# A fused transformer block on one core: two operand stacks filled by halves, feed-forward buffers of their own, distances over 120 quarters

## The reference, cut to what matters

```python
x = x + attn_a(layernorm(x))   # att1: 3 coordinates per token, scores = -distance/4, causal softmax over keys, @ V
x = x + ffn(layernorm(x))      # ffn2: sigmoid(xr Wr) * (relu(xk Wk)^2 Wv), xr and xk mix a token with the one before
x = x + attn_b(layernorm(x))   # proj3 + attention: 16 heads of 16, causal softmax(q k / 4) v
x = x + ffn(layernorm(x))      # ffn4: the same weights as ffn2
```

## Time and profile before

| | us |
|---|---|
| three runs | 2085.45, 2093.70, 2105.44 |
| median | 2093.70 |
| profiled execution, its own time | 2109.85 |
| its span, first to last instruction | 2108.1 |
| PE, DVE, ACT, POOL busy | 1849.2, 1467.0, 1323.7, 728.2 |
| granted clock of TensorE, mean | 0.943 of full speed |

### The profile page before, as it was taken

The page is one execution under the profiler, slowest core; times in us unless marked ns, Lnnn a source line. Parts: engine busy times, 40 slices in busy tenths (PEclk is TensorE's granted clock), DMA queues, the critical chain, the costliest instruction groups (busy, mean ns, idle before and its releaser), DMA issues. The chain is left out here.

```text
span 2108.1 us, 32379 instructions
## 1 busy us (share of the span) xinstructions
PE 1849.2 (88%) x9842; PEld 922.5 (44%) x9842; DVE 1467.0 (70%) x4288; ACT 1323.7 (63%) x2585; POOL 728.2 (35%) x879
## 2 busy tenths in 40 slices
PE   5677898889997999889998899979998899988986
PEld 4453443335543455434543355434544345322423
DVE  5576778767676677667786667766776677768642
ACT  3564355876569565776758665695657766455664
POOL 1342332234333253333443243333532334312313
PEclk8797899999998999999999899989999999989998
DMA  3006113111131112410132111311124101322000
GB/s 85 1 23 123 26 56 67 31 31 32 55 76 31 31 31 82 80 21 12 41 110 42 31 31 56 76 31 31 34 83 76 22 11 41 99 33 50 13 21 20
DMA packets 64346, 97.26 MB, mean 46 GB/s; under 512 B 15655, under 2 KB 58029, under 8 KB 58030
## 3 DMA queue, kind: packets, MB, share of 16 engines
q1 hardware_dynamic: 64174, 95.20, 20.2%
HBM read 61.09 MB, written 33.55 MB: 45 GB/s over the span
## 5 line engine op out<-in xcount | busy, mean ns | idle before, releaser
L973 ACT ACTIVATE pt<-exp_bank 128x512 f32<-128x512 f32 (+1 forms) x1216 | 698.9, 582 | 526.6 <-PE exp_bank L935 521.0
L989 DVE CUSTOM_DVE_ANT_0 max_bank<-max_bank,mask 128x128 f32<-128x128 f32 (+3 forms) x1024 | 501.8, 500 | 400.9 <-PE max_bank L922 386.4
L922 PE MATMUL max_bank<-ks,qs 96*128 96x512 bf16 (+3 forms) x1536 | 523.5, 346 | 85.9 <-DVE piece_max L992 44.9
L935 PE MATMUL exp_bank<-qs,ks 98*128 98x512 bf16 (+3 forms) x1536 | 515.4, 342 | 40.0 <-ACT pt L973 37.0
L992 DVE TENSOR_REDUCE piece_max<-max_bank 128x1 f32<-128x512 f32 x512 | 344.1, 686 | 94.4 <-PE max_bank L922 90.2
L954 PE MATMUL o_bank<-pt,v 128*17 128x512 f32 (+3 forms) x3072 | 334.1, 508 | 13.7 <-POOL pt L1011 11.0
L922 PEld LDWEIGHTS max_bank<-ks,qs 96*128 96x128 bf16 x1536 | 150.9, 99 | 399.5 <-DVE piece_max L989 140.9
L1011 POOL TENSOR_SCALAR_AFFINE_SELECT pt<-pt 128x512 f32<-128x512 f32 x256 | 171.5, 670 | 412.6 <-ACT pt L973 411.8
L935 PEld LDWEIGHTS exp_bank<-qs,ks 98*128 98x128 bf16 x1536 | 152.4, 100 | 236.0 <-ACT pt L973 118.5
L633 PE MATMUL side<-vp,p 128*128 128x260 f32 x576 | 171.4, 423 | 28.7 <-ACT p L560 21.0
L412 ACT ACTIVATE xh<-xs,shift,rstd 128x256 f32<-128x256 f32 x256 | 149.7, 596 | 47.8 <-POOL shift L401 47.8
(11 more groups left out here) (119 smaller groups left out, 2348.4 us busy)
## 6 DMA issues: line engine op xcount, KB each, us to landing
parts_dram<-parts SPq DMA_DIRECT2D x64, 384.0 KB, 2.6
qs<-parts_dram SPq DMA_DIRECT2D x192, 128.0 KB, 7.2
ks<-parts_dram SPq DMA_DIRECT2D x32, 384.0 KB, 4.7
xs<-in_L_attn_a_x_dram SPq DMA_DIRECT2D x16, 512.0 KB, 4.2
ks<-parts_dram SPq DMA_DIRECT2D x32, 256.0 KB, 5.4
out_dram<-xs SPq DMA_DIRECT2D x16, 512.0 KB, 3.1
ks<-parts_dram SPq DMA_DIRECT2D x32, 128.0 KB, 5.8
qs<-neg_maxT SPq DMA_DIRECT2D x64, 8.0 KB, 1.9
```

Source lines behind the costliest of these rows:

```text
L922: pe.matmul(max_bank[u % MAX_BANKS][:, 0:k1 - k0], qs[r][0:KROWS, j, P * tile:P * (tile + 1)], ks[r][0:KROWS, j, k0:k1], start=True, stop= ...
L935: mm = pe.matmul(exp_bank[k % EXP_BANKS][:, (q1 - q0) * slot:(q1 - q0) * (slot + 1)], ks[r][:, j, P * kt:P * (kt + 1)], qs[r][:, j, q0:q1] ...
L973: act.activation(pt[:, e % 2, j + 1 - heads:j + 1, 0:w], exp_bank[k % EXP_BANKS][:, 0:heads * w].rearrange("p (j n) -> p j n", j=heads), A ...
L989: dve.tensor_tensor_reduce(scores, scores, mask[:, HALF - w:HALF], 1.0, LOWEST, ALU.add, ALU.max, piece_max[:, j, m:m + 1]).then_inc(max_f ...
```

## The change

It touches the table, the memory and the DMA queue at once.

- **Two stacks** in place of three. A stack's halves (tokens 0 to 511 and 512 to 1023) are loaded apart, by nine DMAs of half the size each, the first half 16 quarters ahead of the group, the second at its first quarter; PE waits for them at pieces 0 and 4. A run of contiguous bytes in DRAM falls from 8192 to 1024.
- **Maxima by halves**: PE's transposes, DVE's negation and copy and the DMAs come twice per group, after piece 3 and after piece 11, and each half takes eight DMAs in place of one pair for the whole (512 in place of 64). `LEAD` falls from 14 pieces to 12.
- **Feed-forward buffers**: `shifted` (three tensors), and `tm` also holds the gate. The waits between distances and feed-forward go; in their place the first Exp of the gate waits for `x_added`, Relu for the products of the half before.
- **A fourth x buffer**; x is stored and loaded at piece 13 of two turns later (before: 35 of one turn later).
- **The table**: att1 begins 66 quarters earlier, its distances take 120 quarters (`LONG`) from item 2 on; ffn4 begins at 168 in place of 82, but at 82 in the last turn. `XT_BEFORE` gives the wait for the transposed x in the new order. By `place()`, in the steady turn: ffn4 at quarters 4 to 34, ffn2 at 76 to 113, values and positions at 100 to 124, `project` at 139 to 167, distances and `attend` from 116 to 53 of the next turn.
- `p1` is shorter, with a wait before its front is used again. The rows of ones in the stacks are set by POOL instead of DVE. For item 1 the third square is ACT's instead of DVE's.

```diff
-STACKS = 3
+STACKS = 2
-LEAD = NP + 2
+LEAD = NP
-X_BUFFERS = 3
+X_BUFFERS = 4
-ATT1, FFN2, FFN4, PROJ3 = -44, 50, 82, 114
+ATT1, FFN2, FFN4, PROJ3 = -110, 52, 168, 110
+LAST_FFN4 = 82
...
+STACK_AT = [4 * (LEAD - 2 * NP + 2 * TPH), 4 * (LEAD - NP)]
...
-        STAGES += [(TURN * (n - 1) + FFN4, "ffn4", n - 2, 0)]
+        STAGES += [(TURN * (n - 1) + (FFN4 if n < B else LAST_FFN4), "ffn4", n - 2, 0)]
...
-PIECE_TIME = [2 + (q1 - q0) // P for _, q0, q1 in KEY_PIECES] + [5, 5, 5]
-PIECE_AT = [34 + sum(PIECE_TIME[:p]) for p in range(NP + 4)]
+SHORT = [2 + (q1 - q0) // P for _, q0, q1 in KEY_PIECES] + [5, 5, 5]
+LONG = [4 + 2 * (q1 - q0) // P for _, q0, q1 in KEY_PIECES] + [6, 6, 6]
+
+
+def piece_time(n, p):
+    return (SHORT if n < 2 else LONG)[p]
...
-    rows = [(4 * NP * (g + 1) + 1, ("maxima", g)) for g in range(GROUPS)]
+    rows = [(4 * (NP * g + (NP if h else TPH)) + 1, ("maxima", g, h)) for g in range(GROUPS) for h in range(2)]
...
+        shifted = [sb(f"shifted{k}", [P, NC, HALF]) for k in range(3)]
...
-                    if p == 0 and n > 1:
-                        act.wait_ge(tm_ready, 2 * halves_before("att1", n, 0))
...
-                    elif s == "ffn2":
-                        pool.wait_ge(p1_exp, NP * (n + 1))
...
                 if f > 0:
-                    act.wait_ge(ka_ready, 2 * f - 1 + j)
+                    act.wait_ge(v_full, 2 * f)
...
-                r = th[:, 2 * j:2 * j + 2, :]
+                r = tm[:, 2 * j:2 * j + 2, :]
                 if k == 0:
-                    if f > 0:
-                        act.wait_ge(tm_ready, 2 * f - 1 + j)
+                    if f == 0:
+                        act.wait_ge(setup_taken, 5)
+                    else:
+                        act.wait_ge(x_added, 2 * f - 1 + j)
...
             if n > 1:
-                sp_stack(NG * n)
+                for h in range(2):
+                    yield STACK_AT[h] + 4 * NP * NG * n
+                    sp_stack(NG * n, h)
...
-        def sp_stack(group):
+        def sp_stack(group, half):
...
+            lo, hi = HALF * half, HALF * (half + 1)
             if group >= STACKS:
-                nc.sync.wait_ge(s_full, EXP_PER_GROUP * (group - STACKS + 1))
+                nc.sync.wait_ge(s_full, exp_before(NP * (group - STACKS) + (2 * TPH if half == 0 else NP)))
...
-                    to[HD * slot:HD * (slot + count), :, :],
-                    src[kq, ht, part:part + count].rearrange("r d h n -> (r d) h n")[:, h0:h0 + GH, :]
-                ).then_inc(stack_ready[r], 16)
+                    to[HD * slot:HD * (slot + count), :, lo:hi],
+                    src[kq, ht, part:part + count].rearrange("r d h n -> (r d) h n")[:, h0:h0 + GH, lo:hi]
+                ).then_inc(stack_ready[r][half], 16)
...
-                    pe.wait_ge(crow_ready, 32 * (g + 1))
+                    pe.wait_ge(crow_ready, 256 * g + 128)
+                if m == TPH and j == 0:
+                    pe.wait_ge(crow_ready, 256 * g + 256)
...
-            if j == 0 and early == 0 and STACKS <= g < GROUPS and (g % NG or g == NG):
-                sp_stack(g)
+            for half in range(2):
+                g, early = divmod(u - STACK_AT[half], 4 * NP)
+                if early == 0 and STACKS <= g < GROUPS and (g % NG or g == NG):
+                    sp_stack(g, half)
...
             for c in range(2):
-                nc.sync.dma_start(qs[r][KROWS + c:KROWS + c + 1, :, :], neg_maxT[:, c, :]
-                                  ).then_inc(crow_ready, 16)
+                for j in range(GH):
+                    nc.sync.dma_start(qs[r][KROWS + c:KROWS + c + 1, j, HALF * h:HALF * (h + 1)],
+                                      neg_maxT[TPH * j:TPH * (j + 1), c, :]).then_inc(crow_ready, 16)
...
-            for r in range(STACKS):
-                yield SETUP_AT[7] + 12 + 8 * r
-                dve.memset(ks[r][KROWS:SROWS, :, :], 1.0).then_inc(rows_of_ones, 1)
...
+            pool.wait_ge(shift_ready, 2)
+            for r in range(STACKS):
+                pool.memset(ks[r][KROWS:SROWS, :, :], 1.0).then_inc(rows_of_ones, 1)
...
-                body = {"att1": [dve_att1(at, n)] + ([dve_squares(at, n)] if n < 2 else []), "proj3": [dve_proj3(at, n), dve_values3(at, n)]}.get(s, []) if h == 0 else []
+                body = {"att1": [dve_att1(at, n)] + ([dve_squares(at, n)] if n == 0 else []), "proj3": [dve_proj3(at, n), dve_values3(at, n)]}.get(s, []) if h == 0 else []
```

190 lines of the change are left out of this document (96 added, 94 removed).

## The result

| | before | changed |
|---|---|---|
| runs of the first comparison | 2085.45 to 2105.44, median 2089.76 (4) | 2125.89 to 2133.77, median 2127.61 (4) |
| ratio, 95% interval | | 1.0173 [1.0113, 1.0232] |
| profiled execution, its span | 2109.85, 2108.1 | 2125.89, 2124.2 |

The change is slower by 1.7%. The forecast was 2041 us, on the profile's scale 2056.9; the profiled execution took 2125.9, 69 us more.

A forecast was written before the change was run, and what follows sets the result against it. The prediction took ACT to bound the steady turn's first quarter (distances) and PE the rest. Its terms, -57 - 5 - 7 + 8 + 8 = -53, took 2109.85 to 2056.9, or 2041 us on the median's scale; range 1995 to 2095.

The forecast's parts named there:

- That is 8 us a turn, 32 over the four equal turns: Steady turn, cut into four stretches of 48 quarters: PE loads divided by filling give 237.9 us against 245.8 measured.
- The filling of 0.93: Steady turn: PE assumed busy 93% of the second to fourth stretches, giving 57.5 and 60.4 us for third and fourth.
- The last sentence of the prediction: Stretches: the forecast fails above all if filling depends on how distances interleave, not on load; no size given.
- Twice as many transposes of maxima ... +8: PE, per group: 32 new pairs of transposes cost between 0 and 18 us, taken as +8.
- `LEAD` is two pieces shorter ... -5: End of the kernel: the wait for the row of maxima after the last maximum shrinks, -5 us.
- The uneven turns: Groups 2 and 3 +2, 4 to 7 -21, 24 to 27 -17, 28 +11 us.
- Preparation -7: Start: DVE loses three memsets and squares, ACT gets 12 squares; -7 us, between +7 and -25.
- Stores +8: SP's queue: proj3's first store stands behind half a stack and maxima DMAs; 1.3 us for each of six items, +8.
- the 12 us that the rule by itself promised: First stretch: if activity releases the throttle, the whole 4.9 us goes in five turns, some 12 us below the sum.
- B: Rival: stacks and maxima hold back proj3's first store, DVE waits 7.8 us per item, 47 in all; 2080 us, chance 0.21.
- C: Rival: distances keep their price by sharing ACT's queue with the feed-forward, +18 us a turn; 2140 us, chance 0.15.
- A: Rival: PE filled to 98% in all four stretches, 224.6 us a turn; 1976 us, chance 0.12.

The follow-up runs named there:

- e3: The changed kernel with the old table and the old pace of the distances; 2150.4 us, ratio 1.0192 to the kernel before.
- e7: The changed kernel with DVE's subtraction in proj3 done on one column in place of 512; 2126.6 us, against 2129.4 for the changed kernel.
- e13: The changed kernel with DVE's row maxima taken over 128 columns in place of up to 512; 2030.4 us, ratio 0.9661 to the kernel before.
- e1: The kernel before with maxima by halves, still lead 14, three stacks and the old table; 2121.0 us, ratio 1.0070.
- e2: The kernel before with maxima by halves and LEAD 12, still three stacks and the old table; 2141.2 us, ratio 1.0147.
- e12: The kernel before with only two preparation parts: rows of ones set by POOL, item 1's third square on ACT; 2094.0 us, ratio 0.9969.
- e5: The changed kernel with only the first row of maxima written to the stack, four DMAs a half in place of eight; 2123.6 us, ratio 1.0122.
- e6: The changed kernel with ACT's Ln and square root (Exp) of the distances done on one column; 2123.7 us, against 2129.4 for the changed kernel.
- e8: The changed kernel with ACT's squares of the distances of items 2 to 7 done on one column; 2124.8 us, ratio 1.0113 to the kernel before.
- e4: The changed kernel with LEAD 14 again, two stacks kept; 2228.3 us, ratio 1.0559 to the kernel before.
- e14: The kernel before with DVE's row maxima taken over 128 columns in place of up to 512; 2025.5 us, ratio 0.9637.
- e15: The kernel before with ACT's squares of the distances of items 2 to 7 done on one column; 2069.3 us, ratio 0.9848.

## Why the prediction was wrong

On the profile's scale the sum was 69 us short. e3 splits it: 38 in the parts outside the table (+42 by the profiles, +4 forecast), 31 in the table (-26 for -57). Two steps failed. Outside the table it is the price of the shorter lead, put at -5 and measured at +20, the largest single miss. In the table it is the filling of the steady turn, with 16 of the 31 us in the four equal turns (-16 for -32), and nearly all of the rest in turn 6.

- **"That is 8 us a turn, 32 over the four equal turns": the step that failed in the table.** Its loads of PE were right within 1 us, and so was the clock: the turn's PE busy fell from 225.9 to 222.3. ACT's load in the first stretch was not (46.2 for 40.3), but that stretch came out as forecast. The filling of 0.93 for the third and fourth stretch was wrong. It had been read where whole feed-forwards, long matmuls, fill PE. In the new mix of transposes, values and proj3 PE stands for hand-overs (7.2 and 8.7 us of rest for 4.0 and 4.2). That DVE's maxima and side work make part of these rests is shown by e7 and e13; what makes the others is not. The last sentence of the prediction, that filling might depend on how the distances interleave, named this risk, and it came true. Against the old table on the same base the turns gained 1.0 to 6.0 us, against the profile of the kernel before none; e3's equal turns are 23 us longer than those of before, and that is the price of the parts outside the table.
- **"Twice as many transposes of maxima ... +8"**: e1 measured +14, within the bounds of 0 and 18; in it DVE's casts also wait 4.3 us for stores behind the DMAs of the maxima, which the sum had under the stores. In the changed kernel PE rested 15.3 us before 64 pairs, 0.24 each, near the 0.27 of the earlier trace rows; cover for them was the exception:

```profile
L1054 PE MATMUL side<-identb,neg_max 128*16 128x128 bf16 x128 | 18.5, 228 | 15.3 <-DVE neg_max L1022 14.0 <-ACT xt L451 0.9 <-DVE v L869 0.3
```

- **"`LEAD` is two pieces shorter ... -5": the step that failed outside the table.** The gain at the end is right (-5.6), and the chain there has no transfer of maxima, as it had in the earlier trace rows; it goes from the last maximum straight on:

```profile
2051.55 0.60 DVE piece_max L1018
2052.18 0.19 DVE neg_max L1020
2052.39 0.19 DVE neg_max L1022
2052.62 0.28 PE side L1054 x2
2052.90 0.34 PE exp_bank L955
2053.26 1.04 ACT pt L993 x2
```

  What the sum left out is that `LEAD` also sets which maximum runs beside which Exp in all 384 pieces. The shorter lead cost some 26 us inside the turns (e2 less e1 by the medians, with the end's gain added back), and PE's rests before the Exps doubled; that the pairing of wide pieces is the reason is argued, as said above.
- **The uneven turns**: against e3, turn 0 +3.4, 1 -16.7, 6 -1.9, 7 +11.6, for forecasts of +2, -21, -17, +11. Three of four are near. Turn 6 had been credited with the feed-forward that leaves it, and what holds it is DVE: in e13 that turn took 217.4 in place of 234.9.
- **Preparation -7**: the start was 11.0 shorter, inside the bounds, but that is luck: the two parts from which it was added up gave 2.5 in e12. **Stores +8**: 12.0 us of wait, and e5 got 11.3 back behind the start. Here the mechanism was right.
- **The clock.** The Trainium skill ("TensorE: Matmul & The Clock Gate", Part 1) has activity releasing the throttle. The trace agrees in sign: the turn's mean clock rose from 0.96 to 0.99, the first stretch's from 0.91 to 0.95. But the first stretch stayed at 0.95 and didn't reach 1.00, so the 12 us that the rule by itself promised didn't come, and the half of it that the sum took did (PE busy 60.2 for 60.3). The prediction's own reading, 1.00 wherever PE was filled to 94% or more, didn't carry over: the first stretch, filled to 94%, had 0.95, and the third and fourth, at 88 and 86%, had 1.00.
- **Rivals.** B as priced (7.8 us an item) didn't come, only its mild form. C gave the right side and nearly the time (2140), for the wrong reason: PE's rests for ACT's Exps fell, and when e6 and e8 take away what it named, the steady turn stays. A's 1976 us are 150 away.

Still open: what e4's other 70 us are; what else than DVE holds the third and fourth stretch, and whether a fourth side bank or a third max bank would release it (not tried); and the new table with three stacks and lead 14, which wasn't tried either.

## What to carry to other kernels

A stretch's filling is not a number to take from another stretch: before moving work, list the hand-overs (who empties the bank that the moved job needs, and behind what it stands in that engine's order), since behind a bound that is removed at one engine the next one can stand, with buffers just as shallow. An offset such as the lead is part of the schedule of every piece, not only of the drain; price it over all pieces, by what it puts side by side. Take the base from more than one execution: the one profile from which all sums started was slower than every run beside it. And change a table, a lead and a memory plan one at a time: here the table's 26 us were spent, and by the profiles 16 more, on what came with it.

## What the runs showed of the hardware

- An engine at 70% busy can be the one to lighten: 47 us less of DVE a turn brought 7 us or more in both kernels; 11.5 us less of ACT (164.9 to 153.4) brought 7 where a stretch had it at 90%, and 10.5 us less brought none where it was nowhere above 73%.
- A rest that is taken from PE can come back as clock: in e7's fourth stretch PE rested 6.1 us in place of 8.7, at a granted clock of 0.92 in place of 1.00, and the stretch got 1 us longer.
- One kernel has steady turns of different length within one execution, by the clock: 240.9 to 245.8 us in e12 with a first stretch at 0.97 to 0.88, and 245.9 and 250.2 in the changed kernel with a fourth stretch at 1.00 and 0.90. So that quite different edits give the same turn in their profiles (245.8 in the changed kernel and 246 before, 239 in e13, e14 and e15) says little.
- PE kept a granted clock of 1.00 through stretches in which it was busy 86 and 88%, and lost it in one filled to 94% (0.95, the first). The dip there lies at its start, right behind a stretch of rest (3.92 of 6 us), as these rows of the changed kernel show:

```profile
876.00:882.00 6.00, 3.92 (x30) 1.09 (x30) 5.53 (x20) 4.60 (x9) 3.86 (x5) 1.00 0.43 93
882.00:889.00 7.00, 5.74 (x20) 2.42 (x20) 5.53 (x21) 4.78 (x10) 3.06 (x4) 0.52 0.17 35
```

- Copies of 64 KB in runs of 1024 bytes landed after 2.8 us (median of 384), stores of 384 KB after 2.6; nine copies for half a stack were complete 6.4 us after the first issue, nine for a whole one, in runs of 8192 bytes, after 11.6; the DMA share fell from 0.21 to 0.19 a turn, though the packets of the run rose from 64,346 to 112,993.
